# A layer of attention and experts on one core: six small operations of the second attention move from VectorE to GpSimd

## The reference, cut to what matters

```python
def _pool_to_latents(x):                     # 256 rows -> 64 latents, four rows each
    return x.reshape(Bx, N_LATENTS, chunk, C).mean(axis=2)
local  = _local_window_attn(Q, K, V)         # 16 heads, windows of 32
...
# ffn: softmax over 64 experts, the 8 largest weights kept and scaled to sum 1;
# each expert has a capacity of 64 rows; beside them a shared expert
# with a sigmoid gate
y = y.reshape(T, TOP_K, H).sum(axis=1)
return (y + shared).reshape(B, S, H)
```

## Time and profile before

| | |
|---|---|
| median of three runs | 1778.53 us |
| the profiled execution | 1785.13 us |
| its span, first to last instruction | 1783.4 us |
| instructions | 44379 |
| busy over the span: TensorE (PE), VectorE (DVE), ScalarE (ACT), GpSimd (POOL) | 87%, 64%, 57%, 47% |
| mean granted clock of TensorE | 0.950 of full speed |

### The profile page before, as it was taken

One profiled execution on the slowest core, in us unless ns is written; L12 is line 12 of the kernel. 1 busy time (PEld: TensorE's weight loads), 2 busy tenths in 40 slices (PEclk: granted clock), 3 DMA queues, 4 the chain that ended last, 5 costly groups with the idle time before them and its releaser, 6 DMA issues.

```text
span 1783.4 us, 44379 instructions
## 1 busy us (share of the span) xinstructions
PE 1553.7 (87%) x14185; PEld 1132.9 (64%) x14187; DVE 1139.0 (64%) x2695; ACT 1025.2 (57%) x2630; POOL 836.0 (47%) x1415
## 2 busy tenths in 40 slices
PE   4798999999999999998999388888888888885883
PEld 4655555555555555555999277777777777764772
DVE  3345555555555555542444399999999999996661
ACT  3344555555555555553444478878888788862331
POOL 5233455555555555554443544444444544412663
PEclk9998999999999999999999699999999999996666
DMA  7402222222222222223222112121121212116444
GB/s 193 130 12 70 55 55 54 54 54 54 54 54 54 54 54 54 54 58 81 59 65 59 24 42 45 43 44 41 41 45 41 44 41 41 44 34 122 85 85 115
DMA packets 208176, 107.53 MB, mean 60 GB/s; under 512 B 103034, under 2 KB 196539, under 8 KB 208059
## 3 DMA queue, kind: packets, MB, share of 16 engines
q1 hardware_dynamic: 197882, 93.23, 21.0%
q0 software_dynamic: 10240, 13.64, 3.6%
HBM read 61.92 MB, written 40.16 MB: 57 GB/s over the span
## 4 chain that ended last, share of the span: by engine, by line
PE 51%; DVE 20%; issue 12%; DMA 6%; ACT 5%; SPq 3%; POOL 2%; DVEq 1%; POOLq 0%; another core or an unknown queue 0%; ACTq 0%
PE bankB L1827 7%; PE bankA L1775 5%; PE bankT L1810 5%; DVE mxs L1241 5%; DVE pt L1251 4%; PE bankT L1970 4%; PE bankB L1831 3%; PE bankS L1788 3%; PE bankT L1813 2%; PE bankB L1840 2%; PE bankT L1959 2%; PE bankB L2122 2%; PE bankS L1959 2%; DMA remainders<-yT 2%; PE bankS L1793 1%
## 5 line engine op out<-in xcount | busy, mean ns | idle before, releaser
L665 POOL TENSOR_SCALAR_AFFINE_SELECT probs<-probs 128x512 f32<-128x512 f32 x256 | 183.7, 741 | 166.7 <-ACT probs L1451 166.6
L904 DVE TENSOR_REDUCE mneg<-bankS 128x2 f32<-128x256 f32 x256 | 107.5, 420 | 228.2 <-PE bankS L1793 209.5
L1451 ACT ACTIVATE probs<-bankT 128x1024 f32<-128x1024 f32 x128 | 131.1, 1024 | 190.0 <-PE bankT L1813 186.8
L905 DVE TENSOR_REDUCE mneg<-bankS 128x2 f32<-128x512 f32 x256 | 174.6, 682 | 0.0
L1442 ACT ACTIVATE qT<-bankA,bd 128x256 f32<-128x256 f32 x256 | 107.6, 473 | 92.6 <-PE bankA L1775 92.6
L1775 PE MATMUL bankA<-xnT,wd 128*128 128x256 f32 x512 | 152.2, 422 | 0.0
L1810 PE MATMUL bankT<-qT,kT 37*128 37x512 f32 x512 | 140.1, 624 | 7.6 <-DMA qT<-mT 5.8
L658 POOL CAST qb<-qT 128x256 bf16<-128x256 f32 x256 | 97.8, 401 | 100.8 <-ACT qT L1442 100.6
L1827 PE MATMUL bankB<-probs,vaug 128*64 128x512 f32 x512 | 141.4, 631 | 1.1 <-ACT yT L1458 1.0
L1251 DVE STREAM_TRANSPOSE pt<-pe 128x768 f32<-128x768 f32 x128 | 123.7, 967 | 1.6 <-ACT pe L1547 1.6
L1458 ACT COPY yT<-bankB 128x512 f32<-128x512 f32 x128 | 75.1, 586 | 85.2 <-PE bankB L1831 85.2
(11 more groups left out here) (320 smaller groups left out, 4331.6 us busy)
## 6 DMA issues: line engine op xcount, KB each, us to landing
rzb<-reciprocals SPq DMA_DIRECT2D x128, 128.0 KB
yT<-yT SPq DMA_DIRECT2D x64, 128.0 KB
xtab<-tab SPq DMA_DIRECT2D x32, 192.0 KB, 2.0
xs_sorted<-zeros SPq DMA_DIRECT2D x1, 4608.0 KB, 18.4
qT<-xs_sorted SPq DMA_DIRECT2D x36, 128.0 KB, 2.1
ys_sorted<-qT SPq DMA_DIRECT2D x36, 128.0 KB, 1.8
value_rows<-vrow SPq DMA_DIRECT2D x32, 128.0 KB, 1.8
vx<-value_rows SPq DMA_DIRECT2D x256, 16.0 KB, 1.8
```

What stands on the lines that cost most here:

```text
L665: pool.affine_select(out=blocks, in_=blocks, compare_op=ALU.is_ge, fill=0.0, base=0, pattern=[[0, 4], [1, P]], channel_multiplier=-1).then ...
L905: dve.tensor_reduce(mneg[:, n.half, 1, :, j], bankS[:, :, 128:384], AX.X, ALU.max, negate=True).then_inc(S["red_done"], 1)
L1451: act.activation(pT[:, g % 2].rearrange("p e j t -> p e (j t)"), bankT[:, 0:2, :], ACT.Exp, scale=SCALE0).then_inc(S["exp_done"], 1)
```

## The change

`pool_latents`, the sum of the two gated parts, and all of `weigh` but the sum over the experts leave VectorE's list and become instructions of GpSimd. The pooling becomes two additions of neighbours with a tile `xq` between them. The reciprocal becomes a power of -1 with a constant tile `minus`. GpSimd's loop is written as a `step1` of its own with batches p, n, b, m and k. VectorE keeps the sum over the experts as `weight_sum`. Semaphore counts follow; `x1_copied` is folded into `x1_done`, with three counts a batch. The diff, without those counts and the declarations of semaphores:

```diff
+        minus = sb("minus", [P, 1])
+        xq = sb("xq", [P, 2 * NL])
+            pool.memset(minus[:, :], -1.0)
-            with pool.Fori(0, LOOP - 1) as i:
-                for b in (Batch(i, 0), Batch(i, 1)):
-                    stream1(b.next().next())
-                    norm1(b.next().next(), True)
...
+            def pool_latents(n):
+                pool.wait_ge(S["tT_sb"], n.b + 1)
+                passed(pool)
+                pairs = xT1[:, n.half, :].rearrange("p (m k) -> p m k", k=2)
+                pool.tensor_tensor(xq[:, :], pairs[:, :, 0], pairs[:, :, 1], ALU.add).then_inc(S["xp_done"], 1)
+                pool.wait_ge(S["xp_done"], n.b * 2 + 1)
+                pairs = xq[:, :].rearrange("p (m k) -> p m k", k=2)
+                pool.tensor_tensor(xp[:, n.half, :], pairs[:, :, 0], pairs[:, :, 1], ALU.add).then_inc(S["xp_done"], 1)
+
+            def gated_sum(b):
+                pool.wait_ge(S["comb"], b.b * 2 + 2)
+                passed(pool)
+                pool.tensor_tensor(aT[:, :], at1[:, :], at2[:, :], ALU.add).then_inc(S["aT_done"], 1)
+
+            def weigh(n):
+                u = n.half
+                pool.wait_ge(S["ex_done"], n.b + 1)
+                pool.wait_ge(S["M_done"], n.b + 1)
+                passed(pool)
+                pool.tensor_scalar(sgc[:, u, :], tsg[:, :], 0.5, 0.5, ALU.mult, ALU.add)
+                pool.tensor_tensor(exl[:, :, :], exl[:, :, :], mb[:, u], ALU.mult).then_inc(S["rstep"], 1)
+
+            def weights(n):
+                u = n.half
+                pool.wait_ge(S["rstep"], n.b * 3 + 2)
+                passed(pool)
+                pool.tensor_tensor(wsum[:, 1, :], wsum[:, 0, :], minus[:, 0:1].to_broadcast([P, 2]), ALU.pow).then_inc(S["rstep"], 1)
+                pool.wait_ge(S["rstep"], n.b * 3 + 3)
+                pool.tensor_tensor(tab[:, u, :, C:C + E1], exl[:, :, :], wsum[:, 1, :].unsqueeze(2).to_broadcast([P, 2, E1]),
+                                   ALU.mult).then_inc(S["tab_done"], 1)
+
+            def step1(b, p, n, m, k):
+                if n:
+                    pool_latents(n)
+                if m:
+                    stream1(m)
+                if p:
+                    gated_sum(p)
+                if n:
+                    weigh(n)
+                if m:
+                    norm1(m, True)
+                if n:
+                    weights(n)
+                if b:
                     normalise_rows(b)
                     add_stream(b)
-                    gather(b.next().next().next())
-            stream1(Batch(LOOP, 0))
-            norm1(Batch(LOOP, 0), True)
-            normalise_rows(Batch(LOOP - 1, 0))
-            add_stream(Batch(LOOP - 1, 0))
-            gather(Batch(LOOP, 1))
-            stream1(Batch(LOOP, 1))
-            norm1(Batch(LOOP, 1), True)
-            normalise_rows(Batch(LOOP - 1, 1))
-            add_stream(Batch(LOOP - 1, 1))
-            normalise_rows(Batch(LOOP, 0))
-            add_stream(Batch(LOOP, 0))
-            normalise_rows(Batch(LOOP, 1))
-            add_stream(Batch(LOOP, 1))
+                if k:
+                    gather(k)
+
+            first, second = Batch(0, 0), Batch(0, 1)
+            gather(first)
+            gather(second)
+            clear()
+            stream1(first)
+            norm1(first, False)
+            stream1(second)
+            pool_latents(first)
+            weigh(first)
+            norm1(second, False)
+            weights(first)
+            gather(Batch(1, 0))
+            step1(first, None, second, Batch(1, 0), Batch(1, 1))
+            step1(second, first, Batch(1, 0), Batch(1, 1), Batch(2, 0))
+            with pool.Fori(1, LOOP - 1) as i:
+                step1(Batch(i, 0), Batch(i, 0).before(), Batch(i, 1), Batch(i + 1, 0), Batch(i + 1, 1))
+                step1(Batch(i, 1), Batch(i, 0), Batch(i + 1, 0), Batch(i + 1, 1), Batch(i + 2, 0))
+            step1(Batch(LOOP - 1, 0), Batch(LOOP - 2, 1), Batch(LOOP - 1, 1), Batch(LOOP, 0), Batch(LOOP, 1))
+            step1(Batch(LOOP - 1, 1), Batch(LOOP - 1, 0), Batch(LOOP, 0), Batch(LOOP, 1), None)
+            step1(Batch(LOOP, 0), Batch(LOOP - 1, 1), Batch(LOOP, 1), None, None)
+            step1(Batch(LOOP, 1), Batch(LOOP, 0), None, None, None)
+            gated_sum(Batch(LOOP, 1))
...
-
-            def pool_latents(n):
-                dve.wait_ge(S["tT_sb"], n.b + 1)
-                dve.tensor_reduce(xp[:, n.half, :], xT1[:, n.half, :].rearrange("p (n k) -> p n k", k=CHUNK), AX.X,
-                                  ALU.add).then_inc(S["xp_done"], 1)
-
-            RSTEPS = 4
 
             def route(n):
                 u = n.half
@@ -1211,8 +1251,8 @@
                 passed(dve)
                 for t in range(2):
                     ins = dve.max(mx8[:, t, :], lg1[:, t, 0:E1])
-                ins.then_inc(S["rstep"], 1)
-                dve.wait_ge(S["rstep"], n.b * RSTEPS + 1)
+                ins.then_inc(S["top8"], 1)
+                dve.wait_ge(S["top8"], n.b + 1)
                 passed(dve)
                 for t in range(2):
                     ins = dve.match_replace(lgr[:, t, :], mx8[:, t, :], lg1[:, t, 0:E1], NEG)
@@ -1220,19 +1260,10 @@
                 dve.wait_ge(S["ex_in"], n.b + 1)
                 dve.tensor_tensor(mb[:, u], lg1[:, :, 0:E1], lgr[:, :, :], ALU.not_equal).then_inc(S["M_done"], 1)
 
-            def weigh(n):
-                u = n.half
-                dve.wait_ge(S["ex_done"], n.b + 1)
-                dve.wait_ge(S["M_done"], n.b + 1)
-                dve.tensor_tensor(exl[:, :, :], exl[:, :, :], mb[:, u], ALU.mult).then_inc(S["rstep"], 1)
-                dve.wait_ge(S["rstep"], n.b * RSTEPS + 2)
+            def weight_sum(n):
+                dve.wait_ge(S["rstep"], n.b * 3 + 1)
+                passed(dve)
                 dve.tensor_reduce(wsum[:, 0, :], exl[:, :, :], AX.X, ALU.add).then_inc(S["rstep"], 1)
-                dve.wait_ge(S["rstep"], n.b * RSTEPS + 3)
-                dve.reciprocal(wsum[:, 1, :], wsum[:, 0, :]).then_inc(S["rstep"], 1)
-                dve.wait_ge(S["rstep"], n.b * RSTEPS + 4)
-                dve.tensor_scalar(sgc[:, u, :], tsg[:, :], 0.5, 0.5, ALU.mult, ALU.add)
-                dve.tensor_tensor(tab[:, u, :, C:C + E1], exl[:, :, :], wsum[:, 1, :].unsqueeze(2).to_broadcast([P, 2, E1]),
-                                  ALU.mult).then_inc(S["tab_done"], 1)
 
             def shift(b, g):
                 k = g % 2
@@ -1276,8 +1307,6 @@
                 dve.scalar_tensor_tensor(at1[:, :], tg[:, u, 0, :], 1.0, rowsT[:, 0:T], ALU.add, ALU.mult).then_inc(S["comb"], 1)
                 dve.wait_ge(S["rem2_ps"], b.b + 1)
                 dve.scalar_tensor_tensor(at2[:, :], tg[:, u, 1, :], 1.0, rem_ps, ALU.add, ALU.mult).then_inc(S["comb"], 1)
-                dve.wait_ge(S["comb"], b.b * 2 + 2)
-                dve.tensor_tensor(aT[:, :], at1[:, :], at2[:, :], ALU.add).then_inc(S["aT_done"], 1)
 
             def finish(b):
                 u = b.half
@@ -1286,8 +1315,6 @@
                 dve.tensor_tensor(res[:, u], out_rows_ps, res[:, u], ALU.add).then_inc(S["res_done"], 1)
 
             def step1(b, p, n, m):
-                if n:
-                    pool_latents(n)
                 if b:
                     shift(b, 1)
                 if p:
@@ -1311,7 +1338,7 @@
                 if b:
                     turn(b, 3)
                 if n:
-                    weigh(n)
+                    weight_sum(n)
                 if b:
                     shared_gated(b)
                     shared_hidden(b)
@@ -1552,7 +1579,7 @@
                 act.copy(xT1[:, n.half, :], bank[0][:, 0:T]).then_inc(S["tT_sb"], 1)
 
             def xp1(n):
-                act.wait_ge(S["xp_done"], n.b + 1)
+                act.wait_ge(S["xp_done"], n.b * 2 + 2)
                 act.copy(xpr[:, n.half], xp[:, n.half, :].rearrange("p (n q) -> p n q", q=W).unsqueeze(2).to_broadcast([P, 2, 4, W])).then_inc(S["xpr_sb"], 1)
 
             def spread(dst, src):
```

More of the change, by code:

```diff
@@ L304, in program @@
         rstep M_done ex_in ex_done tab_done cnt_ps cnt_sb v_ps v_sb s2_ps red2 sub_done exp2 tr_done shg_ps shu_ps tanh_sh
-        sh1_done sh_sb shd_ps av_ps rd_done rows_turned rem2_ps v_out v_in0 v_in1 rows_sb gate_ps gate_sb comb aT_done scaled x1_copied ao_ps r1_done res_done
+        sh1_done sh_sb shd_ps av_ps rd_done rows_turned rem2_ps v_out v_in0 v_in1 rows_sb gate_ps gate_sb comb aT_done scaled top8 ao_ps r1_done res_done
         tab_out0 tab_out1 res_out0 res_out1 l1_consts wprep xpr_sb slots cnt_out cnt_in0 cnt_in1 owner_done picked_ps sel sidx_done tokf_done diag_done row_done same_done first_done mg_done ym_sb xg_in0 xg_in1
@@ L774, in stream1 @@
                 ins.then_inc(S["x1_done"], 1)
-                pool.wait_ge(S["x1_done"], n.b * 2 + 1)
+                pool.wait_ge(S["x1_done"], n.b * 3 + 1)
                 passed(pool)
@@ L798, in norm1 @@
                     pool.wait_ge(S["tT_ps"], n.b - 1)
```

(8 more changed lines are left out.)

## The result

| | before | changed |
|---|---|---|
| median of four runs | 1776.88 us (1773.74 to 1780.68) | 1906.01 us (1902.40 to 1912.72) |
| the profiled execution, its span | 1785.13, 1783.4 us | 1902.40, 1900.6 us |
| TensorE's mean granted clock over the span | 0.950 | 0.903 |

The ratio is 1.0731 (95% interval 1.0695 to 1.0767): 7.3% slower, 129 us. The forecast was 1915 us, in a range of 1854 to 1958.

A forecast was written before the change was run, and what follows sets the result against it. VectorE, 95% busy, was taken as the full engine, with a nearly as tight chain behind it. Loop of 21.5 plus clock 1.7 gives 23.2 us; 29 x (23.2 - 18.48) = 137 us, on 1778.53: 1915 us, range 1854 to 1958.

The forecast's parts named there:

- The order, not the load: In GpSimd's in-order list the pooling stands behind the gather, four microseconds late; the gated sum stands behind stream1.
- Two loops, nearly equal: Through GpSimd's gather, pooling and gated sum each close a loop, 21.5 and 21.2 us a step; the longer counts.
- The first: Loop from ScalarE's L1556 through keys, TensorE's attention, slots, GpSimd's rows and gather to the pooling: 21.5 us a step.
- The second: Loop from VectorE's L1286 through GpSimd's normalising, gather, landing, gate, stream and gated sum to the output projection: 21.2 us.
- The prices on GpSimd: The moved operations add together about 4 us a step on GpSimd, on top of 8.6 busy.
- The clock: TensorE pauses and falls to 1.2 GHz in most steps, adding 1.7 us: 23.2 us a step.
- The added waits: VectorE's wait for GpSimd's mask has 0.9 us to spare and costs nothing; the later table store on SyncE costs nothing.
- The total: Second attention: 29 steps growing from 18.48 to 23.2 us, 137 us in all, giving 1915 us.
- If VectorE stayed the bound, that would be the gain: VectorE loses some 1.6 us of issue a step, so 18.48 would become 16.9 us.
- the faster rival: The pooling on GpSimd is not late and VectorE's relief remains: 29 x 1.6 = 46 us, 1732 us; 4%.
- the second chain: Behind VectorE, TensorE waits for ScalarE's key copies and GpSimd for ScalarE's rows: nearly as tight as VectorE.

The follow-up runs named there:

- The best kernel here: Changed kernel with the gather moved into GpSimd's idle time and TensorE's remote part behind the next projections: 1756.53 us, ratio 0.9894.
- the two kernels with one loop each: Changed kernel with pooling back on VectorE and eight idle products: 1883.77 us; with gated sum back and five idle products: 1863.00 us.

## Why the prediction was right

- **The order, not the load.** Right. The pooling starts when L768 ends, ScalarE waits 3.6 us (four were forecast), VectorE waits 4.3 us at the residual (3 to 4 were), and moving the gather alone takes the whole loss back.
- **Two loops, nearly equal.** Right: with either one undone, the other still holds the step at 21 us or more. I summed 21.5 and 21.2 us; they measure 21.0 each, together 21.08. The first was mis-sized by 0.5 us. Some 0.2 of it is the pooling, 1.0 in the sum and 0.77 in the timeline (1421.00 to 1421.77), the rest small terms. The second can be followed in the step shown above, from the residual at 1365.58 to the next at 1386.56: 6.33 us to L792, 2.82 to the end of the normalising, 1.15 for power and product (1.5 in the sum), 5.14 to the end of the gather, 1.79 to the landing, 2.19 for gate and stream, 0.68 for the sum and 0.88 to the residual. That path is tight at full clock only: in the changed kernel GpSimd, done with power and product, still waits for ScalarE's rows in front of L819 (40.6 us in 28 times; 8.1 in 28 where idle products hold the clock up). A small misreading: the prediction called GpSimd busy "without a pause" at the end of its step, but 0.82 and 0.30 us of the gather's 3.55 are idle, before the two L765; the sum has them right.
- **The prices on GpSimd.** Near: 0.41 and 0.29 us for the two additions, 0.43 and 0.40 for mask and product, 0.71 for the power, 0.72 for the sum, against 0.45, 0.33, 0.45, 0.45, 0.73 and 0.73. From the 4497 ns that the Trainium skill gives for an add of 2048 elements (GPSIMD Engine Reference, performance versus the Vector engine) the estimate is 2.2 ns an element. By it the step from 64 to 128 elements should be 0.14 us; it is 0.12.
- **The clock.** Right that it falls in each step; the size is right by luck. 1.7 us a step were forecast, and 22.74 - 21.08 = 1.66 were measured. But it was worked out with a mean clock of 0.76, where 0.85 was measured, and on 5.5 us of TensorE's work. With 0.85 the same formula gives 5.5 x (1/0.85 - 1) = 1.0 us. The stretch was too short as well: the falls also cover the output projection (L2155 takes 1.22 us above, 0.66 in the earlier trace rows) and the scores and the gate in front of the attention. Two errors cancelled.
- **The added waits.** Right: VectorE's sum over the experts does not appear among the waits. SyncE waits 1.1 us a step for the table's product (L465 for L850), but then it waits 10.5 us more for the residual (L475) anyway, so the table's store holds nobody up.
- **The total.** 23.2 us a step against 22.74, and 29 steps against 28, make the growth 137 us against 118, 19 us too much. The forecast is off by only 9 us, because the medians lie 129 us apart and not 117. That closeness is luck too; the step's 22.74 us lie in the forecast 22.3 to 24.3.
- **What was wrong** stood beside the forecast: "If VectorE stayed the bound, that would be the gain: 18.48 - 1.6 = 16.9 us a step", and with it the 1732 us of the faster rival. With the order mended the step is 18.13, not 16.9. I had named the second chain as "nearly as tight" and then left it out of this rival's price. The best kernel here, with that chain opened too, has 17.53.

## What to carry to other kernels

An engine that is idle for half of its time has room only where it is idle. Before moving work to it, find the work's place in the engine's in-order list, and what stands in front of that place. Slow instructions that nobody waits for soon, such as a gather for a later batch, belong in the engine's own idle time and never ahead of work that is due. Where two loops are nearly equal, undoing one of them leaves the other, so test by removing what they share. And look at TensorE's clock wherever a new wait makes it pause: at how long it is low, and at which work lies under it.

## What the runs showed of the hardware

- Idle products of TensorE paid for themselves: two groups a step, busy for 1.35 and 1.31 us, took the step from 22.74 to 21.08 us, with the clock up from 0.85 to 1.00. With other counts in the two kernels with one loop each they did not hold the clock fully (0.94 and 0.98), and the second of these got no faster.
- What a fall of the clock costs depends on the work under it: in the two kernels with the gated sum back on VectorE, steps with a fall near the latent and output projections took 21.0 to 21.4 us, steps with a fall in the middle of the attention 22.5 to 23.0.
- Each of the two indirect DMAs of a step holds GpSimd itself (1.10 and 0.96 us in the timeline above), and the next instruction started only behind them (1420.02 + 0.96 = 1420.98, then L826 at 1421.00).
- GpSimd takes 0.71 us for a power of two elements per partition and 0.72 for an addition of 256: an operation's kind can outweigh its size there.
- With GpSimd's work up, VectorE's instructions kept their length: L1276 takes 957 to 960 ns in the changed kernel, as L1245 did before.
